# Keys' squares folded on GpSimd before VectorE sums them, with another order on VectorE and the shifted inputs made in three parts

## What is computed

```
def shift_tokens(t):
    a, s = jnp.split(t, 2, -1)
    s = jnp.pad(s, ((0, 0), (1, 0), (0, 0)))[:, :-1]
    return jnp.concatenate([a, s], -1)

def l2norm(t):
    return t / jnp.maximum(jnp.linalg.norm(t, axis=-1, keepdims=True), 1e-12)

qkv = shift_tokens(x) @ Wqkv                 # 16 heads of 64
q, k = l2norm(q) * qs, l2norm(k) * ksc       # norm over the 64 of a head
q, k = rotary(q), rotary(k)
attn = softmax(mask(q @ k.T * 8))            # within 32 tokens
out  = (attn @ v) @ Wo
x = out + x
x = ffn(shift_tokens(x)) + x
```

## Time and profile before

| | us |
|---|---|
| median of 3 runs | 2846.3 |
| lowest, highest | 2845.92, 2847.65 |
| the profiled execution | 2847.98 |
| its span in the trace | 2846.2 |

### The profile page before, as it was taken

One profiled execution on the slowest core, in us unless ns is written; L12 is line 12 of the kernel. 1 busy time (PEld: TensorE's weight loads), 2 busy tenths in 40 slices (PEclk: granted clock), 3 DMA queues, 4 the chain that ended last, 5 costly groups with the idle time before them and its releaser, 6 DMA issues.

```text
span 2846.2 us, 92826 instructions
## 1 busy us (share of the span) xinstructions
PE 2691.9 (95%) x36416; PEld 2060.1 (72%) x36417; DVE 2600.1 (91%) x3375; ACT 2246.7 (79%) x3776; POOL 2116.7 (74%) x1529
## 2 busy tenths in 40 slices
PE   8799978999999999999999999999999999999996
PEld 7577756777777777777777777777777777777774
DVE  7899968999999999999999999999999999999993
ACT  5799957878788787878888787888878787887873
POOL 6766658777778777778777787777787777877771
PEclk9899999999999999999999999999999999999998
DMA  1000013232223332223232232222322322322222
GB/s 57 24 2 2 1 35 76 67 76 69 67 69 75 73 73 66 69 71 75 66 79 69 66 75 71 72 67 70 76 67 68 79 62 68 72 67 58 64 66 79
DMA packets 103719, 178.41 MB, mean 63 GB/s; under 512 B 29350, under 2 KB 52708, under 8 KB 103396
## 3 DMA queue, kind: packets, MB, share of 16 engines
q1 hardware_dynamic: 102372, 174.60, 25.2%
q10 hardware_dynamic: 1152, 1.20, 0.1%
HBM read 22.62 MB, written 2.10 MB: 9 GB/s over the span
## 4 chain that ended last, share of the span: by engine, by line
PE 30%; POOL 16%; issue 15%; ACT 11%; DMA 7%; DVE 5%; SPq 1%; POOLq 0%; ACTq 0%; DVEq 0%
PE pa L843 9%; POOL spare L1446 8%; DMA kT<-spare 7%; PE px L872 5%; PE pg L982 3%; PE ps L903 3%; PE pg L960 3%; PE px L917 3%; PE pg L974 2%; POOL xs_lo L1432 2%; DVE ss L1269 2%; ACT spare L1095 2%; POOL pr L1484 2%; ACT spare L1041 1%; POOL spare L1455 1%
## 5 line engine op out<-in xcount | busy, mean ns | idle before, releaser
L1446 POOL TENSOR_TENSOR spare<-spare,qk_t 128x1024 f32<-128x1024 f32 x384 | 910.1, 2392 | 10.9 <-POOL xs_lo L1432 8.1
L843 PE MATMUL pa<-w_hi,xs_hi 128*128 128x512 f32 x1152 | 511.9, 444 | 25.3 <-issue 8.6
L1462 POOL TENSOR_TENSOR sm<-sm,inv 128x512 f32<-128x512 f32 x192 | 201.8, 1051 | 429.2 <-DVE sm L1307 361.4
L1285 DVE TENSOR_TENSOR qk_t<-pa,rot 128x1024 f32<-128x1024 f32 x384 | 464.6, 1210 | 1.6 <-ACT spare L1048 0.8
L1276 DVE TENSOR_TENSOR spare<-pa,rot 128x1024 f32<-128x1024 f32 x384 | 464.6, 1210 | 0.0
L1269 DVE TENSOR_REDUCE ss<-spare 128x16 f32<-128x1024 f32 x384 | 457.7, 1192 | 6.1 <-ACT spare L1041 5.2
L843 PE MATMUL pa<-w_hi,xs_lo 128*128 128x512 f32 x1152 | 459.2, 399 | 0.3 <-DMA pT<-prT 0.3
L843 PE MATMUL pa<-w_lo,xs_hi 128*128 128x512 f32 x1152 | 455.0, 395 | 0.0
L872 PE MATMUL px<-ident_sb,spare 128*128 128x128 f32 x3072 | 407.2, 276 | 18.8 <-POOL spare L1455 11.9
L1455 POOL TENSOR_TENSOR spare<-spare,inv 128x1024 f32<-128x1024 f32 x192 | 365.9, 1905 | 69.6 <-ACT inv L1080 65.3
L872 PEld LDWEIGHTS px<-ident_sb,spare 128*128 128x128 f32 x3072 | 340.4, 140 | 105.1 <-issue 44.6
(11 more groups left out here) (178 smaller groups left out, 5926.1 us busy)
## 6 DMA issues: line engine op xcount, KB each, us to landing
kT<-spare SPq DMA_DIRECT2D x384, 256.0 KB, 3.7
pT<-prT SPq DMA_DIRECT2D x768, 64.0 KB, 2.0
w_part<-in_Wqkv SPq DMA_DIRECT2D x40, 192.0 KB, 3.7
wo<-in_Wo SPq DMA_DIRECT2D x6, 512.0 KB, 5.5
c_h<-in_x SPq DMA_DIRECT2D x4, 512.0 KB, 9.5
spare<-in_x SPq DMA_DIRECT2D x8, 256.0 KB, 4.8
out<-spare SPq DMA_DIRECT2D x8, 256.0 KB, 2.5
wo<-in_W SPq DMA_DIRECT2D x6, 341.0 KB, 5.2
```

Source lines behind the costliest of these rows:

```text
L843: last = pe.matmul(pa[(u + c) % 2][:, half * 512:half * 512 + 512], x[:, j * P:(j + 1) * P], w[:, at], start=(k == 0), stop=(k == 2))
L1285: dve.tensor_tensor(halves(qk_t[:, c, :]), halves(pa[(3 * j + c) % 2][:])[:, :, ::-1, :], table.unsqueeze(1).to_broadcast([P, HEADS, 2, DH ...
L1446: pool.tensor_tensor(qk_r[:, c, :], qk_r[:, c, :], qk_t[:, c, :], ALU.add)\
```

## The change

Four edits.

1. GpSimd gets a new step, `fold_squares_k`, first in every turn: it adds the upper 32 squares of each head to the lower 32, in place in `sq`, after `square_k`. `sum_squares` becomes two functions: `sum_squares_q` is as before, `sum_squares_k` waits for the fold and sums 32 elements of a head.
2. On VectorE `sum_squares_q` moves from behind `turn_probs` to ahead of it.
3. On VectorE the reciprocal of the denominators leaves `denominators`; in turns 0 to 2 it stands behind `rest_of_outputs`, in the last turn where it was.
4. The shifted input is made in three parts, of 256, 128 and 128 tokens. The last tile's part is made in the group's first turn; the third tile's goes to the last turn of the group before, on ScalarE behind the copy of qT and on GpSimd behind `norm_keys`. TensorE waits for them in the turns 0, 2 and 3.

```diff
-        HALF_TOK = 2 * P
+        SHIFT_PART = ((0, 2 * P), (2 * P, P), (3 * P, P))
...
-                        if j % 2 == 0:
-                            pe.wait_ge(s["xs_ready"], 4 * i + j + 2)
+                        if j != 1:
+                            pe.wait_ge(s["xs_ready"], 6 * i + (2 if j == 0 else 2 * j))
...
-                        wait_for(act, s["v_full"], g * GT - 2 * (1 - half))
+                        wait_for(act, s["v_full"], g * GT - (2 - part))
...
                         if j == 0:
-                            shift_hi(i, 0, 1)
-                        if j == 2:
-                            shift_hi(i, -1, 0)
+                            shift_hi(i, 0, 2)
+                        if j >= 2:
+                            shift_hi(i, -1, j - 2)
...
+                def sum_squares_k(i, j, back):
+                    n, j, live = tile(i, j, back)
+                    if live:
+                        dve.wait_ge(s["folded_k"], n + 1)
+                        wait_for(dve, s["floored"], n)
+                        dve.reduce_sum(ss[:, 1, :], heads(sq)[:, :, 0:DH // 2], AX.X).then_inc(s["sum_k"], 1)
...
                         maximum(i, j, 2)
+                        sum_squares_q(i, j, 0)
                         turn_probs(i, j, 3)
-                        sum_squares(i, j, 0, 0, "sq_q", "sum_q")
...
-                        sum_squares(i, j, 0, 1, "sq_k", "sum_k")
+                        sum_squares_k(i, j, 0)
...
                         denominators(i, j, 2)
+                        if j == 3:
+                            reciprocals(i, j, 2)
                         rest_of_outputs(i, j, 3)
+                        if j < 3:
+                            reciprocals(i, j, 2)
...
+                def fold_squares_k(i, j, back):
+                    n, j, live = tile(i, j, back)
+                    if live:
+                        pool.wait_ge(s["sq_k"], n + 1)
+                        low, high = heads(sq)[:, :, 0:DH // 2], heads(sq)[:, :, DH // 2:DH]
+                        pool.tensor_tensor(low, low, high, ALU.add).then_inc(s["folded_k"], 1)
...
                     for j in range(GT):
+                        fold_squares_k(i, j, 0)
                         norm_scores(i, j, 2)
...
                         if j == 0:
-                            shift_lo(i, 0, 1)
+                            shift_lo(i, 0, 2)
+                        if j == 3:
+                            shift_lo(i, -1, 1)
```

More of the change, by code:

```diff
@@ L1133, in tables, with shift_hi @@
                         act.preload_act_table_set(name)
-                def shift_hi(i, back, half, first=False):
+                def shift_hi(i, back, part, first=False):
                     g, live = group(i, back)
@@ L1259, in _ @@
                         shift_hi(0, 0, 1, True)
+                        shift_hi(0, 0, 2, True)
                 group_steps(act, body, lambda l: None)
@@ L1424, in _, with shift_lo @@
             def _(pool):
-                def shift_lo(i, back, half, first=False):
+                def shift_lo(i, back, part, first=False):
                     g, live = group(i, back)
@@ L1428, in shift_lo @@
                     if live:
-                        at = bass.ds((g % GROUPS) * GTOK + half * HALF_TOK, HALF_TOK)
-                        to = slice(half * HALF_TOK, (half + 1) * HALF_TOK)
-                        chunk = 2 * g + half
+                        first_tok, toks = SHIFT_PART[part]
+                        at = bass.ds((g % GROUPS) * GTOK + first_tok, toks)
+                        to = slice(first_tok, first_tok + toks)
+                        chunk = 3 * g + part
                         rest = lambda dst, src: pool.tensor_tensor(dst, src, hi, ALU.subtract)
@@ L1530, in _ @@
                 shift_lo(0, 0, 1, True)
+                shift_lo(0, 0, 2, True)
                 pool.wait_ge(first_loaded, 3 * 16)
```

16 lines of the change are left out of this document (10 added, 6 removed).

## The result

The changed kernel takes 2870.64 us (median of 4 runs, 2864.79 to 2872.91), the kernel before 2846.98 us beside it. The ratio on record is 1.0068, with a 95% interval of 1.0052 to 1.0085: slower by 0.7% (the two medians by themselves are 0.8% apart). 2858 was forecast, so the sign is right and the loss is about twice the size: 2870.64 lies above the band of 2852 to 2868 that went with the forecast, and nearer to the 2876 of the rival of late probabilities than to 2858.

What follows compares the result with a forecast made beforehand. TensorE was taken to set the pace, held by the keys' DMA (first turn) and GpSimd's norm_keys (third). Loop groups 9.0, first groups 0.9, third 1.8: +11.7 us on the 2846.3 median, forecast 2858 (2852 to 2868; rivals 2831 to 2876).

Steps and rivals of the forecast that it cites:

- the rival of late probabilities: Probabilities' DMAs meet the keys' DMA on SyncE's queue or land 0.5 us later: 0.7 a group, 2876 us; chance 0.13.
- The fold's duration: GpSimd's add of 512 elements takes 1.30 us, priced from w_lo's rows; bounds 1.05 and 1.45.
- The fold's path: Second turn: fold makes norm_scores 0.71 late, norm_keys 0.34; TensorE's key transposes of the third turn +0.25 us a group.
- What the new order of VectorE costs: sum_squares_q ahead of turn_probs: first turn's probabilities land 1.1 us later, TensorE 0.1 late (0 to 0.3); second just at need.
- The prediction's own sign of being wrong: Forecast is wrong if the period falls below 49.4, or if TensorE waits in turns where the prediction has none.
- The split: Shifted input in three parts: ScalarE and second turn's scores 0.2 us earlier, TensorE 0.37, then lost waiting for GpSimd.
- VectorE is full but follows: VectorE, busy 46.8 of 49.4 us a group, is no bound: it waits 0.47 us for scores at the group's head.
- The rival of a binding VectorE: VectorE or the keys' DMA sets the pace: TensorE's 0.37 us stays won, 15.5 us in all, 2831 us; chance 0.20.
- The rest of the sum: Groups at each layer's head: first 6 x 0.15 = 0.9 us, second 0, third 6 x 0.3 = 1.8.

## Why the prediction was right, and where it was not

- **The fold's duration** was right: 1.30 us from the two w_lo rows, 1.287 measured. By the Trainium skill ("GPSIMD Engine Reference", section 3.1: 2.6 cycles of 1.2 GHz an element for a two-input add) the estimate was 1.11 us; the measurement decides for the rows. Its section 4.1, which sends such work to VectorE, held in the second turn and not in the third: there the fold was free (period 49.38 with it, 49.39 without).
- **The fold's path** was right in turn, engine and row: norm_scores, norm_keys, the keys' transposes of the third turn. There +0.25 was worked out and +0.38 measured (24.43 instead of 24.05). That taking out the fold gives back 0.23 is no confirmation of the 0.25: by the prediction's own working the kernel without the fold would have kept 0.37 us of gain, so the fold was priced at some 0.6, and it is chance that the two numbers agree. The 0.13 that is missing at the row comes from square_k, which was to start 0.3 us earlier and started 0.1 earlier (13.40 instead of 13.50), so that norm_scores was 0.89 late instead of 0.71. TensorE's wait for norm_keys grew by 22 us over the span where 10 to 15 were named.
- **The failed step is "What the new order of VectorE costs".** The landing times were worked out well in the first turn (3.95; measured 4.01) and 0.2 early in the second (15.5; measured 15.70: turn_probs moved by 1.0 and not by 0.9). The first turn was priced at 0.1 for TensorE and cost 0.26, close to the upper end of 0.3; TensorE swallowed it, but of the 0.2 us that ScalarE was to win and half keep it kept nothing, which is what made square_k and the fold's path late. The second was called "just at its need" and priced at zero: 15.5 was worked out, and the matmul that asks for the probabilities started at 15.57 in the kernel before (1054.37). It cost 0.22 a group where no fold covers it, as much as the fold adds. A margin of under 0.1 us with 0.2 us of error in it is no zero. The prediction's own sign of being wrong, waits of TensorE in turns where it had none, was there: the 32.6 us for the probabilities. The rival of late probabilities had this mechanism, at 0.13, with 2876 us, though by another cause (a meeting of DMAs, or a landing 0.5 us later than worked out).
- **The split** was right in its first effect (scores −0.25 against −0.2, transposes −0.41 against −0.37) and right that it does not last, but wrong in what ends it: in the second turn already, ScalarE's copy of qT, not norm_keys.
- **"VectorE is full but follows" was wrong for the kernel before.** The argument was that VectorE waits 0.47 us for scores at the group's head. But behind that maximum stands turn_probs, and its input from GpSimd comes 0.16 us before it: the wait of the one hides the other. For the changed kernel the reading holds, since the folds shorten VectorE's ring while TensorE's grew; VectorE idles there at 1052.45 and 1062.03. The rival of a binding VectorE was thus neither right nor empty: of the 2 us a group that VectorE saves 0.18 were to be had, and not by this change.
- **The rest of the sum.** The six first groups of the layers were to lose 0.9 us together, the second ones nothing, the third 1.8; they lost 2.7, 1.5 and −0.2. These groups differ by 1 us and more between the layers of one run (the second ones of the changed kernel take from 49.56 to 52.68), so none of the three is clear of it; the loss of the first ones is the steadiest, in four layers of six. The start's 2.4 us and the drain's 5.4 were in no term. Starts range from 397.2 to 399.7 over the kernels here. So the 24.9 us between the profiled executions are a loss per group that was underestimated, some 17 in the layers, and the rest outside them, most of it a drain that does not follow the change.

## What to carry to other kernels

When several edits around a bound leave the period unchanged to 0.02 us, suspect a second ring of the same length, and write one round of it out as durations and handovers. The sum always gives the period; if every handover in it is a short one (0.07 to 0.16 us here) and nothing in between waits, it binds too. A wait that ends an engine's idle time says nothing on the instruction behind it, whose own input may come at the same moment; only moving the first shows the second. A delay that one engine swallows may be passed on by another that reads the same result: follow each reader. An edit that helps in one turn of an unrolled loop and hurts in another should be made in the one turn: the same four edits gave +0.7% everywhere and −0.5% where each was free.

## What the runs showed of the hardware

In the drain TensorE's granted clock falls, and not always for as long. The last 60 us of the profiled run of the changed kernel and, in the second fence, of the kernel before (the granted clock, as a share of 2.4 GHz, is the third figure from the end):

```profile
2799.00:2803.00 4.00, 2.73 (x73) 1.76 (x71) 0.54 (x1) 3.26 (x6) 1.46 (x2) 1.00 0.52 111
...
2807.00:2811.00 4.00, 3.22 (x11) 1.67 (x6) 1.89 (x3) 0.69 (x1) 1.05 (x1) 0.50 0.16 36
...
2811.00:2871.00 60.00, 41.41 (x231) 24.86 (x230) 16.61 (x24) 14.30 (x18) 1.05 (x1) 0.70 0.28 77
```

```profile
2786.00:2846.00 60.00, 39.63 (x300) 24.50 (x300) 19.78 (x29) 16.28 (x20) 2.84 (x3) 0.82 0.29 80
```

Up to 2803 the clock is at its upper level, 2.4 GHz, with TensorE busy 2.73 of 4 us as the work runs out; from 2807 to 2827 it is at the lower, 1.2 GHz, and then changes between the two. The kernel before shows 4 us at a time between 0.57 and 1.00 there, and none at 0.50. The last group and the drain take 119.6 us in the one and 114.3 in the other. It does not follow the change: the kernel with the fold in the third turn has 120.4 us, with a mean of 0.70 over its last 60, and the one with the fourth turn's fold besides 113.3, with 0.81. Why the clock falls longer in one execution than in another stays open. Such a spread of 5 us between single executions is 0.2% of the time, as much as some of the effects studied here, and a reason to compare periods of the loop and not spans.

In the later groups the last of the probabilities' four DMAs lands, on average, 3.88 us behind the end of turn_probs in the kernel before and in those with the new order alone, with the three parts alone and with the reciprocal moved, and 3.93 us in all others: with either order of VectorE, and also in the changed kernel without the fold. What these others share is that their programs declare the fold's semaphore; why their DMAs land 0.05 us later is not shown. And VectorE's sum of 512 elements took 0.67 us against 1.20 for 1024: the fold saves it 0.53 and costs GpSimd 1.29, so GpSimd's time has to be free for it.
